# A greedy planner in place of fixed time shares, and two buffers for the sums of projections

## The reference, cut to what matters

```
x = layernorm(x + self_attention(x, causal))              # layer 0; 16 heads of 8
x = layernorm(x + cross_attention(x, context))            # 1601 keys
x = layernorm(x + moe(x))                                 # 8 experts, 128 -> 512 -> 128, gelu, top 2
x = x + self_attention(rmsnorm(x), mask)                  # layer 1
x = x + cross_attention(rmsnorm(x), context, mask)        # 1601 keys
x = x + shared(rmsnorm(x)) + moe(rmsnorm(x))              # 8 experts and a shared one, silu, top 2
```

## Time and profile before

| | us |
|---|---|
| median of 3 runs | 5363.61 |
| lowest, highest | 5334.2, 5365.39 |
| the profiled execution | 5339.86 |
| its span, first to last instruction | 5338.6 |

### The profile page before, as it was taken

One profiled execution on the slowest core, in us unless ns is written; L12 is line 12 of the kernel. 1 busy time (PEld: TensorE's weight loads), 2 busy tenths in 40 slices (PEclk: granted clock), 3 DMA queues, 4 the chain that ended last, 5 costly groups with the idle time before them and its releaser, 6 DMA issues.

```text
span 5338.6 us, 103443 instructions
## 1 busy us (share of the span) xinstructions
PE 4796.2 (90%) x41312; PEld 2705.7 (51%) x41312; DVE 3578.7 (67%) x8383; ACT 2789.2 (52%) x5505; POOL 639.8 (12%) x660
## 2 busy tenths in 40 slices
PE   5888888888888888888899999999999999999999
PEld 2455455555544555555455544554455544554456
DVE  4666666666566666666767777677777777677774
ACT  1565565666565566655554444444444444444444
POOL 1111111111111111111110111101010111001000
PEclk7799999999898999998999999999999999999999
DMA  2122212222221222222232222322232222322222
GB/s 60 35 46 46 51 46 54 56 58 47 46 51 40 59 55 59 46 50 63 70 79 74 71 64 75 81 72 61 68 77 74 73 61 76 81 69 62 68 60 66
DMA packets 167993, 327.11 MB, mean 61 GB/s; under 512 B 25656, under 2 KB 76624, under 8 KB 167520
## 3 DMA queue, kind: packets, MB, share of 16 engines
q1 hardware_dynamic: 167520, 320.49, 24.5%
HBM read 237.40 MB, written 4.19 MB: 45 GB/s over the span
## 4 chain that ended last, share of the span: by engine, by line
PE 73%; DVE 16%; ACT 5%; issue 2%; SPq 2%; POOL 1%; DMA 1%; DVEq 0%
PE sums L701 13%; PE a L765 10%; PE d L777 10%; PE a L672 9%; PE a L664 7%; DVE chunk_max L809 5%; DVE d L817 4%; ACT probs_c L973 3%; PE d L587 3%; PE d L685 3%; PE a L647 2%; PE d L739 2%; PE d L607 2%; PE a L614 2%; PE d L638 2%
## 5 line engine op out<-in xcount | busy, mean ns | idle before, releaser
L973 ACT ACTIVATE probs_c<-a 128x512 f32<-128x512 f32 (+1 forms) x3584 | 1833.2, 563 | 2032.2 <-PE a L672 2030.2
L817 DVE CUSTOM_DVE_ANT_0 d<-d,mcross_q 128x404 f32<-128x404 f32 x2048 | 1138.7, 605 | 321.0 <-PE d L685 318.1
L809 DVE TENSOR_REDUCE chunk_max<-d 128x2 f32<-128x808 f32 x1024 | 1005.1, 997 | 284.7 <-PE d L685 276.3
L701 PE MATMUL sums<-probs_c,vc 128*32 128x256 f32 x13312 | 1102.6, 404 | 0.2 <-ACT probs_c L973 0.2
L672 PE MATMUL a<-qc,kc 25*128 25x256 f32 (+1 forms) x6656 | 912.3, 336 | 128.2 <-ACT probs_c L973 97.3
L672 PEld LDWEIGHTS a<-qc,kc 25*128 25x128 f32 (+1 forms) x6656 | 531.7, 184 | 813.8 <-issue 410.3
L685 PE MATMUL d<-kc,qc 24*128 24x404 f32 x4096 | 896.9, 451 | 35.3 <-DVE chunk_max L809 17.6
L777 PE MATMUL d<-w_back,hidden 128*128 128x128 f32 x4352 | 559.0, 283 | 36.9 <-DVE chunk_max L817 36.9
L777 PEld LDWEIGHTS d<-w_back,hidden 128*128 128x128 f32 x4352 | 531.4, 196 | 74.7 <-DVE chunk_max L817 50.2
L765 PE MATMUL a<-xT_e,w_in 128*128 128x256 f32 x2176 | 564.7, 405 | 0.0
L664 PE MATMUL a<-mcross_k,ident_b 128*128 128x512 bf16 (+1 forms) x1792 | 539.0, 373 | 13.5 <-ACT probs_c L973 12.6
(11 more groups left out here) (157 smaller groups left out, 4358.3 us busy)
## 6 DMA issues: line engine op xcount, KB each, us to landing
w_in<-in_experts SPq DMA_DIRECT2D x272, 256.0 KB, 3.2
w_back<-in_experts SPq DMA_DIRECT2D x272, 256.0 KB, 2.9
kc<-k_hi SPq DMA_DIRECT2D x1024, 50.0 KB
ctxT<-in_ctxT SPq DMA_DIRECT2D x32, 800.5 KB, 4.5
kc<-k_lo SPq DMA_DIRECT2D x512, 50.0 KB
mask_words<-in_mcross SPq DMA_DIRECT2D x32, 800.5 KB
mask_words<-in_mcrossT SPq DMA_DIRECT2D x32, 768.0 KB
out_x<-xe SPq DMA_DIRECT2D x32, 128.0 KB, 1.8
```

The costliest lines, as they stand in the source:

```text
L701: last = pe.matmul(acc[HP * j:HP * j + HP, :], T["vc"][x.p][0:x.kn, v0:v0 + HP], probs_of(T, x)[0:x.kn, j, half:half + S], start=x.j == 0, ...
L809: done = dve.tensor_reduce(T["chunk_max"][:, x.g % 2, x.i, x.j:x.j + 2, x.c], tile[:].rearrange("p (h n) -> p h n", h=2)[:, :, 0:CHUNK], A ...
L817: done = dve.tensor_tensor_reduce(some, some, mask, 1.0, -3e38, ALU.add, ALU.max, T["chunk_max"][:, x.g % 2, x.i, x.j + h, x.c:x.c + 1])
L973: act.activation(probs_of(T, x)[0:x.kn, x.j, 0:n], tile[0:x.kn, 0:n], ACT.Exp, scale=SCALE).then_inc(M["a_read"], 1)
```

## The change

`weave` no longer sorts by place. It now builds the order step by step: in each turn it takes the first piece of every list whose inputs have been placed and whose place is at most 30 us ahead of the soonest, tries each on a copy of a `Model` of the engines, and appends the one with the least (idle time of PE or DVE in the model + 0.05 x its place in us). The model keeps for each engine the time at which it is free, and the times at which the tiles of both rings come free; `FILL` and `DRAIN` hold assumed durations of the writing and the reading side of each step. The shares of the round and `COST` still give the places. A `WV` and the beat behind it are now two pieces. `q_sum` becomes a pair of tiles used by turns: DVE waits only for the split before the last one. Every engine runs the same instructions as before; only their order, the waits and the second tile differ.

```diff
-def weave(*lists):
-    keyed = []
-    for which, (begin, end, steps) in enumerate(lists):
...
+class Model:
...
+    def add(self, x):
...
+        if x.kind in D_RING or x.kind in A_RING or x.kind == "WV":
+            ring = self.d if x.kind in D_RING else self.a if x.kind in A_RING else [0]
+            begin = max(self.pe, first, ring[0])
+            idle = begin - self.pe
+            self.pe = begin + self.cost(FILL, x)
+            if x.kind in D_RING:
+                second = max(second, self.splits[0]) if x.kind == "QP" else second
+                idle += max(0, second - max(self.dve, self.pe))
+                self.dve = done = max(self.dve, self.pe + HOP, second) + drain
+                self.d = [self.d[1], done + HOP]
...
+NEAR, AHEAD = 0.05, 30.0
+
+def weave(model, length, *lists):
...
+    while any(queues):
+        soonest = min(queue[-1][0] for queue in queues if queue)
+        best = None
+        for which, queue in enumerate(queues):
+            if not queue or queue[-1][0] > soonest + AHEAD:
+                continue
+            place, piece = queue[-1]
+            own = {id(x) for x in piece}
+            if any(id(y) in pending - own for x in piece for y in x.of.values()):
+                continue
+            trial = Model(model)
+            idle = sum(trial.add(x) for x in piece)
+            if best is None or idle + NEAR * place < best[0]:
+                best = idle + NEAR * place, which
...
@@ attention @@
-                    out.append(sums + beat_of(steps))
+                    out += [sums] if sums else []
+                    out.append(beat_of(steps))
@@ vector_program @@
-            if x.n >= 1:
-                dve.wait_ge(M["q_made"], x.n)
-            dve.tensor_tensor(T["q_sum"][:], tile[:].rearrange("p (g s) -> p g s", g=NG),
+            if x.n >= 2:
+                dve.wait_ge(M["q_made"], x.n - 1)
+            dve.tensor_tensor(T["q_sum"][x.n % 2][:], tile[:].rearrange("p (g s) -> p g s", g=NG),
@@ pool_program @@
+            q_sum = T["q_sum"][x.n % 2]
             pool.wait_ge(M["d_read"], in_ring(x))
+            if x.n:
+                pool.wait_ge(M["q_made"], x.n)
```

More of the change, by code:

```diff
@@ L125, in spaced @@
     return [(x, cost_of(x) + (0 if isinstance(x, list) else LATER.get(x.kind, 0))) for x in steps]
-def weave(*lists):
-    keyed = []
-    for which, (begin, end, steps) in enumerate(lists):
+DRAIN = {"QP": 1.3, "KC": 2.65, "VC": 1.0, "SV": 0.5, "MS": 1.2, "NS": 0.45, "NC": 0.45, "MC": (1.0, 1.4), "OT": 0.9,
+         "OPM": 0.45, "RT": (1.2, 1.6), "EBM": 0.45, "ES": 0.6, "SC": 0.6, "SS": 0.6, "WS": 0.4, "XT": 0.4, "OPT": 0.4,
+         "EF": (0.9, 0.6), "EBT": 0.3, "NR": 0.3, "LN1": 1.0, "RM1": 0.7, "MK": 1.2, "R2": 1.8, "R3": 1.5, "LN2": 2.7,
+         "RM2": 1.6, "RS": 0.8}
@@ L134, in weave @@
+NEAR, AHEAD = 0.05, 30.0
+def weave(model, length, *lists):
+    queues = []
+    for begin, end, steps in lists:
         timed = spaced(steps)
-        total, done = sum(cost for _, cost in timed), 0.0
+        total, done, queue = sum(cost for _, cost in timed), 0.0, []
         for x, cost in timed:
-            keyed.append((begin + (end - begin) * (done + cost_of(x) / 2) / total, which, len(keyed), x))
+            place = length * (begin + (end - begin) * (done + cost_of(x) / 2) / total)
+            if isinstance(x, list) or x.kind != "PAUSE":
+                queue.append((place, x if isinstance(x, list) else [x]))
@@ L138, in weave @@
             done += cost
-    return [x for _, _, _, x in sorted(keyed, key=lambda k: k[:3])]
-def flat(order):
+        queues.append(queue[::-1])
+    pending = {id(x) for queue in queues for _, piece in queue for x in piece}
     out = []
-    for x in order:
-        out += x if isinstance(x, list) else [x]
-    return [x for x in out if x.kind != "PAUSE"]
+    while any(queues):
[12 more added lines that the diff above has]
+                best = idle + NEAR * place, which
+        if best is None:
+            raise ValueError("steps wait for each other")
+        _, piece = queues[best[1]].pop()
+        for x in piece:
+            model.add(x)
+            pending.discard(id(x))
+        out += piece
@@ L149, in beat_of @@
+    return out
 def beat_of(steps):
@@ L1158, in program @@
         "qs": sb("qs", [P, NG, S], F32R), "ks": sb("ks", [P, NG, S], F32R), "qc": pair("qc", [P, NG, S], F32R),
-        "q_sum": sb("q_sum", [P, NG, S]), "q_high": sb("q_high", [P, NG, S], F32R),
+        "q_sum": pair("q_sum", [P, NG, S]), "q_high": sb("q_high", [P, NG, S], F32R),
         "mself_q": sb("mself_q", [P, QT, S], BF16), "mself_k": sb("mself_k", [P, QT, S], BF16),
```

75 lines of the change are left out of this document (67 added, 8 removed).

## The result

| | before | change |
|---|---|---|
| median, us | 5348.84 (6 runs) | 5309.62 (6 runs) |
| lowest, highest | 5334.2, 5365.39 | 5302.74, 5326.08 |
| profiled execution | 5339.86 | 5307.29 |
| its mean granted clock | 0.956 | 0.925 |

The ratio of change to before is 0.9928, with an interval of [0.9902, 0.9955]. That is faster by 0.7%, under the 1% that the prediction took as its bound. I had forecast 5205 us, 3.0% less than before. The change gave a quarter of that.

The account below looks back on a forecast made before the run. PE, busy 4796.2 of 5338.6 us, was taken as the bound, with waits to win back: layer 0 -43, layer 1 -48, clock -38, start -10, together -139 from 5339.86, so 5201, stated as 5205 us; range 5060 to 5345.

Parts of the forecast that it names:

- the clock: Layer 0: fewer waits shorten the half-clock stretches that follow idle ones, 2.5 us a round, -38 us (bounds 0 and -132).
- The rival on the slow side: Router steps in one lump make PE wait for DVE in both layers, 7.3 us a round: 5427 us; chance 0.10.
- The waits in layer 0: PE's waits in a layer 0 round fall by 2.9 us in sum, -43 us over 15 rounds.
- Score tiles and bare beats: Layer 0: separated score pairs lose their waits, -3.3 us a round; six more beats without side work cost +1.2.
- Projections: Layer 0, place 1: waits of 3.5 us a round become 2.6, so -0.9 (bounds -2.2 and 0).
- Router: Layer 0, places 2 and 3: waits around `NS` and `EBT` total 3.5 us against 2.9, +0.6 (bounds -1 and +4.3).
- The rival that needed 4.5 us: Slower, by the router: decides from 4.5 us a round of waits at `NS`, `EBT` and nearby maxima; chance 0.10.
- Transfers: Loads move past each other in SP's queue by a beat or two; no PE wait beyond the first load names one.
- The pair of `q_sum` tiles: Keeps adjacent `QP` steps free of POOL; by itself worth little, as DVE waited for POOL's split only 5.3 us.
- Layer 1: Waits at `SV`, the sixth expert's `ES` and others shrink: -3 us a round (bounds 0 and -5), -48 over 16 rounds.
- The start: Ahead of round 0, two `VC` steps move into the wait for POOL's normalization: -10 us (0 to -15).
- The waits only move: Rival: waits that leave one place return at the next; both layers together give -20, 5320 us; chance 0.20.

Follow-up runs that it names:

- fill_g01: The change plus a useless 512-column matmul ahead of the scores in each beat of layer 0's first two head groups: 5180.25 us, ratio 0.9692 to before.
- fill_tiny: The change plus a useless matmul of only 8 columns ahead of the scores in every layer 0 beat: ratio 0.9876 to before.
- fill_g23: The change plus a useless 512-column matmul ahead of the scores in each beat of layer 0's last two head groups: 5288.54 us, ratio 0.9896 to before.
- new_l0: New order in layer 0's rounds, old order in layer 1's, two `q_sum` tiles: 5392.99 us, ratio 1.004 to before.
- near_05: The change with the weight on place raised from 0.05 to 0.5, nearer the old order: 5247.99 us, ratio 0.9797 to before.
- pair_only: The kernel before, in its old order, with two `q_sum` tiles and nothing else: 5340.89 us, ratio 0.9948 to before.
- new_l1: Old order in layer 0's rounds, new order in layer 1's, two `q_sum` tiles: 5252.78 us, ratio 0.9781 to before.

## Why the prediction was wrong

**The step that failed is the clock.** I wrote -38 us, with bounds of 0 and -132, from "the low stretches follow idle ones" and from one pair of rows. It was outside its own bounds, on the other side. The time at half clock in 300 to 2500 us rose from 283 to 509 us, and the mean clock there fell to 0.88 where I had named 0.95 to 0.96 as the sign of being right. Taken by rounds: idle time fell by 4.3 us, the round grew by 4.8, so the busy time grew by 9.1 on 19.2 more us of half clock. Rounds 11 and 12 of the change give a price from one order, 14.3 us on 37.5, which is 0.38 for each; by it the clock took 7.3 of the 9.1 us, and what the other 1.8 are stays open. Over the 15 rounds that makes 110 to 136 us lost to the clock where I had put a gain of 38. Without it the change would have taken some 5171 to 5197 us (an estimate), and fill_g01, which only holds the clock in half of the round, took 5180.

The reasoning failed in its cause. Idle time goes ahead of some low stretches, but a round of the change with 14.8 us of it can be at half clock for 58 us (and one with 15.8 for 20.5). The trace of before had this already. Its rounds 8 and 11 by windows, columns as in Rows 2:

```profile
1339.19:1500.38 161.19, 142.58 (x1227) 83.08 (x1227) 98.82 (x156) 93.61 (x185) 23.11 (x23) 0.88 0.22 49
1817.66:1971.29 153.63, 133.44 (x1227) 79.86 (x1227) 98.56 (x156) 93.39 (x185) 23.10 (x23) 0.96 0.23 52
```

The longer one idles less (18.6 us, and 20.2) and has more low clock (38.1 us, and 13.7), so idle time doesn't say how much of a round runs low. fill_tiny has less idle time than the change and the same clock; fill_g23 and fill_g01 have nearly the same idle time and clocks of 0.90 and 0.96. What raised the clock in the new order, at about the same idle time, was more full-width work in the first half of the round. Whether it has to be full-width is not shown: no run tried 512 columns with few rows of the array. The upper bound of 0 for this term left out a loss, and nothing in the trace of before excluded one. The rival on the slow side needed the clock, not the router.

That the time still lies inside my range is luck: a layer 0 that got slower and a layer 1 that gained twice the forecast (+69 and -92 us) largely cancel.

The Trainium skill (TensorE: Matmul & The Clock Gate, A second HAM failure mode: psum-queue depth-cycling) says of another kernel that frequent micro-idles between groups of matmuls made the clock swing between its two levels. If that held here, fewer waits should mean a higher clock. The runs here don't bear it out as the deciding cause: 19.8 us of idle time a round went with 19.1 us low, 15.5 with 38.3.

**The waits in layer 0** were right in sign and somewhat low: -2.9 us forecast, -4.3 measured, and -5.5 by new_l0, whose trace misses no record.
- Score tiles and bare beats: -3.3 + 1.2 = -2.1 forecast; (84.4 - 114.2) / 14 = -2.1 measured.
- Projections: 2.6 us of waits forecast. L702 has none, `SV`'s maxima wait 0.51 (forecast 0.5), `OT`'s 0.45 (0.3), and those behind the keys' product 0.88 (DVE's k_lo, 12.3 / 14; I had 1.3): 1.8 together.
- Router: I had 3.5 us. `NS` itself waits 0.1 (I had 0.85), the maxima behind it 1.16, `EBT` 0.67, the next maxima 0.15 (2.1 / 14): 2.1 us. The rival that needed 4.5 us is refuted.
- Transfers: I said that none would be named. The load of the first expert's weights is, 15.3 us in 14 waits, 1.1 a round. I had put the moves of the loads past each other at nothing.

**The pair of `q_sum` tiles** was mis-sized: nothing by itself in my sum, 0.5% measured. I took the profile's 5.3 us for all of DVE's wait for POOL.

**Layer 1** was right in its places and too small: -3 us a round forecast, -7.8 measured (170.7 to 162.9), beyond my bound of -5. Idle time gives 4.5 of it, and 3.3 come from closer packing inside the busy time, which I had not priced because I counted only gaps. About 1 us a round is the pair's (15 us in 15 rounds). Of the 7.8 x 15 = 117 us that steady rounds would give, 92 arrived: the round in which the layers meet took most of the rest (180.3 us with 38 us at half clock, where before it had 167.5).

**The start**: -10 forecast, -13 measured, with some luck: new_l0, which starts in the same order, gained 11, and near_05 7. **"The waits only move"** has the nearest time (5320), but not the mechanism: they went. The Trainium skill's reading of repeated gaps (Perfetto Trace Analysis, Optimization Strategy), too few buffers for the next tile, held for a small part: the second `q_sum` tile took 1.3 us of idle time out of a layer 1 round (10.7 to 9.4 in pair_only). The order, with the same rings, took out another 3.2 (new_l1).

**What stays open.** Why the same order gives rounds of 153.6, 160.6 or 167 us: a low stretch begins 21 us into the round and lasts 3.4, 20 or 34 us (in some of the 160.6 it begins at 31 and lasts 17). What the clock answers to: less full-width work stands in the first half, and near_05 says that lumps matter, but no run took one list alone, and none changed the width of the filler. Whether 256 columns are better than 128, and why the old order gets nothing from the filler.

## What to carry to other kernels

On a PE that is 90% busy a new order can lose more to the clock than it wins by closing gaps (here 110 us or more against some 65 in layer 0). Before pricing a new order by waits, list the stretches at half clock with what PE does in them, and give the clock term a bound on both sides: here an order with fewer gaps lowered the clock. Compare rounds of the same kernel first, as two of one order can show what the clock alone costs. As a test, and where it pays as a cure (it did not in the old order), put useless full-width matmuls into a tile that will be overwritten anyway, with a few-column version as the control and one half of the loop at a time. Test each part of a change alone: here the second buffer alone gave 0.5% where both parts gave 0.7%, and the order was slower than before without it.

## What the runs showed of the hardware

- PE stayed at half clock for 34.1 us while it was busy 94% of the time (2017.98 to 2052.10), mostly with matmuls of 24 to 32 rows or columns, and eight sums that took 0.64 us at full clock took 1.08.
- 896 extra matmuls of 512 bf16 columns made the changed kernel 2.8% faster and the kernel before 1.4% slower; with 8 columns they left the clock at 0.88.
- The same instructions in the same order took 153.6 or 167.5 us in two successive rounds.
- A wait on two semaphores was put down to the wrong engine: 32.3 us named PE and were POOL's.
